# Attention scores from stacked float32r halves in two row groups instead of three bfloat16 parts, with smaller stack transfers and later expert loads

## The reference

```python
q, k, v = proj(Wq, bq), proj(Wk, bk), proj(Wv, bv)          # 16 heads x 2048 x 8
scores = einsum('bhqd,bhkd->bhqk', q, k) * (1 / sqrt(8))     # causal mask: -inf where k_pos > q_pos
p = softmax(scores);  out = einsum('bhqk,bhkd->bhqd', p, v) @ Wo.T + bo
x = layernorm(x + out)
x = layernorm(x + moe(x) + shared(x))                        # fp32 throughout
```

## Time and profile before

| what | value |
|---|---|
| median of 3 runs | 677.12 us (675.03 to 679.25) |
| span of the profiled execution | 662.1 us |
| PE busy | 559.1 us, 84% |
| DVE busy | 468.2 us, 71% |
| ACT busy | 356.9 us, 54% |
| mean granted TensorE clock | 0.914 of full speed |

### The profile page before, as it was taken

The page is one execution under the profiler, slowest core; times in us unless marked ns, Lnnn a source line. Parts: engine busy times, 40 slices in busy tenths (PEclk is TensorE's granted clock), DMA queues, the critical chain, the costliest instruction groups (busy, mean ns, idle before and its releaser), DMA issues.

```text
span 662.1 us, 10390 instructions
## 1 busy us (share of the span) xinstructions
PE 559.1 (84%) x3497; PEld 237.3 (36%) x3497; DVE 468.2 (71%) x765; ACT 356.9 (54%) x803; POOL 151.3 (23%) x267
## 2 busy tenths in 40 slices
PE   6244812999976999999999999999999899999890
PEld 3122401343422333344333333333333323665360
DVE  6933810789974898888888888788885333676674
ACT  2000301566551777767777777776778797332250
POOL 9600210221211022020101010110101325425453
PEclk9755765899995999999999999999999999999996
DMA  3221453000210000211000000000000101222133
GB/s 87 76 116 51 123 126 108 2 2 1 94 81 21 2 2 1 70 82 47 1 2 0 2 2 1 2 1 1 2 1 2 35 25 29 59 41 60 33 65 91
DMA packets 22204, 25.61 MB, mean 39 GB/s; under 512 B 2282, under 2 KB 20658, under 8 KB 21570
## 3 DMA queue, kind: packets, MB, share of 16 engines
q1 hardware_dynamic: 20192, 21.67, 10.2%
q0 software_dynamic: 1536, 3.15, 2.5%
q10 hardware_dynamic: 424, 0.13, 0.1%
HBM read 17.44 MB, written 7.21 MB: 37 GB/s over the span
## 4 chain that ended last, share of the span: by engine, by line
PE 67%; DVE 9%; SPq 7%; DMA 6%; issue 4%; POOL 3%; ACT 1%; POOLq 0%; DVEq 0%; ACTq 0%
PE out_ps L1291 20%; PE ring_ps L1274 17%; PE score_ps L1250 17%; SPq L619 5%; DMA k_stack<-parts_dram 4%; DVE part_max L986 3%; PE score_ps L1380 2%; PE score_ps L1253 2%; PE ring_ps L1397 1%; PE ring_ps L1300 1%; DVE qk_parts L965 1%; POOL k_stack L809 1%; DVE qk_parts L967 1%; PE score_ps L1332 1%; SPq L610 1%
## 5 line engine op out<-in xcount | busy, mean ns | idle before, releaser
L986 DVE TENSOR_REDUCE part_max<-score_ps 128x2 f32<-128x1024 f32 (+3 forms) x320 | 327.7, 1062 | 115.3 <-PE score_ps L1253 82.7
L863 ACT ACTIVATE probs<-ring_ps 128x512 f32<-128x512 f32 (+3 forms) x611 | 285.1, 537 | 157.0 <-PE ring_ps L1274 154.8
L1250 PE MATMUL score_ps<-k_stack,q_stack 96*128 96x512 bf16 (+3 forms) x640 | 183.7, 366 | 41.3 <-DMA k_stack<-parts_dram 29.2
L1274 PE MATMUL ring_ps<-q_stack,k_stack 96*128 96x512 bf16 (+3 forms) x611 | 173.5, 354 | 28.1 <-DMA q_stack<-max_rows 26.4
L1291 PE MATMUL out_ps<-probs,v_aug 128*32 128x512 f32 (+3 forms) x1280 | 153.5, 552 | 3.7 <-POOL probs L730 3.2
L1250 PEld LDWEIGHTS score_ps<-k_stack,q_stack 96*128 96x128 bf16 x640 | 60.9, 102 | 131.7 <-issue 58.8
L1274 PEld LDWEIGHTS ring_ps<-q_stack,k_stack 96*128 96x128 bf16 x611 | 52.6, 99 | 141.9 <-ACT probs L863 69.8
L730 POOL TENSOR_SCALAR_AFFINE_SELECT probs<-probs 128x512 f32<-128x512 f32 x64 | 40.6, 634 | 189.5 <-ACT probs L863 189.2
L1253 PE MATMUL score_ps<-mask_qk,ident_bf 128*128 128x128 bf16 x256 | 56.8, 241 | 0.0
L1291 PEld LDWEIGHTS out_ps<-probs,v_aug 128*32 128x32 f32 x1280 | 25.5, 109 | 49.7 <-issue 24.2
L741 POOL CAST max_parts<-row_max 128x16 bf16<-128x16 f32 x48 | 9.4, 196 | 146.1 <-DVE row_max L994 144.1
(11 more groups left out here) (179 smaller groups left out, 427.4 us busy)
## 6 DMA issues: line engine op xcount, KB each, us to landing
q_stack<-parts_dram SPq DMA_DIRECT2D x3, 1152.0 KB
k_stack<-parts_dram SPq DMA_DIRECT2D x9, 384.0 KB
parts_dram<-qk_parts SPq DMA_DIRECT2D x8, 384.0 KB, 2.5
sorted_dram<-q_stack SPq DMA_DIRECT2D x30, 64.0 KB, 1.5
x_sb<-in_L_attn_x_dram SPq DMA_DIRECT2D x4, 256.0 KB, 5.1
w_gu<-n_L_ffn_expert_gate_dram SPq DMA_DIRECT2D x1, 1024.0 KB, 26.6
w_gu<-in_L_ffn_expert_up_dram SPq DMA_DIRECT2D x1, 1024.0 KB, 11.7
wd<-n_L_ffn_expert_down_dram SPq DMA_DIRECT2D x8, 128.0 KB, 3.3
```

Of the source, the lines that this page charges most:

```text
L863: act.activation(probs[:, n % RING, 0:w], bank(it)[:, 0:w], ACT.Exp, scale=SCALE).then_inc(probs_ready, 1)
L986: dve.tensor_reduce(out=part_max[:, s % 2, t, 2 * hp:2 * hp + 2, c], in_=score_ps[:, m % 2, :, 0:w], axis=AX.X, op=ALU.max).then_inc(score ...
L1250: last = mm(score_ps[:, m % 2, i, 0:w], q_stack[0:KROWS, B % 2, h, t * P:(t + 1) * P], k_stack[0:KROWS, c, h, 0:w], start=True, stop=c < B)
L1274: mm(bank(it)[:, 0:w], k_stack[0:KROWS, j // TPB, h, j % TPB * P:(j % TPB + 1) * P], q_stack[0:KROWS, B % 2, h, skip:BLK], start=True, sto ...
```

## The change

- q and k are split into two float32r halves (ACT the first, DVE the second at once with one instruction, L962 before and L951 now); all 2 x 2 products make 32 rows, plus one row of -1 and two rows of maxima: 33 rows for the scores, 35 for the probabilities.
- Two heads share a stack row: head 2u in rows 0 to 63, head 2u + 1 in rows 64 to 127 (HALF = 64). The tensors keep their size in bytes per partition (8 pairs x 512 x 4 bytes).
- The two matmuls of a job read rows 0.. and rows 64..; the two mask matmuls of a masked job now come behind both.
- Stack transfers: q in four of 16 rows, k in two of 32 rows; each send is two transfers of 64 rows. Row maxima are placed with four transfers in place of one.
- Expert weights are loaded one expert at a time, three transfers behind the maxima of steps 5 to 13.
- The maxima are split in two steps on POOL, not five, and turned in float32.
- Rows read later by the mixture of experts (x1T, xs) lie elsewhere; three waits on q_sent and k_sent protect them.

```diff
-PARTS = 3
+HALVES = 2
+EXPERT_LOADS_AT = 5
-            clock["tensor"] += 0.84 * w + 8 + 107 * (c == B)
+            clock["tensor"] += 0.42 * w + 8 + 107 * (c == B)
...
-        q_stack = sb("q_stack", [P, 2, H, BLK], BF16)
-        k_stack = sb("k_stack", [P, NB, H, BLK], BF16)
+        q_stack = sb("q_stack", [P, 2, PAIRS, BLK], F32R)
+        k_stack = sb("k_stack", [P, NB, PAIRS, BLK], F32R)
...
-                sp.wait_ge(q_sent[b], 16)
-                rows = parts_dram[0, b].rearrange("a (o d h) t -> o (a d) h t", o=1, d=HD)[:, :, heads, :]
-                sp.dma_start(q_stack[0:STACK, b % 2, heads, :].rearrange("p h t -> p (h t)"),
-                             rows.rearrange("o p h t -> o p (h t)").to_broadcast(
-                                 [PARTS, PARTS * HD, (heads.stop - heads.start) * BLK])).then_inc(stacked, 16)
+                sp.wait_ge(q_sent[b], 32)
+                columns = slice(pairs.start * BLK, pairs.stop * BLK)
+                for j in range(2):
+                    for r in range(HALVES):
+                        at = HALF * j + r * HALVES * HD
+                        sp.dma_start(q_stack[at:at + HALVES * HD, b % 2, pairs, :].rearrange("p u t -> p (u t)").bitcast(F32),
+                                     parts_dram[0, b, j].rearrange("a d e -> d a e")[:, :, columns]).then_inc(stacked, 16)
...
+                for j in range(2):
+                    rows = parts_dram[1, b, j].rearrange("a (d o) e -> (a d) o e", o=1)[:, :, pairs.start * BLK:pairs.stop * BLK]
+                    sp.dma_start(k_stack[HALF * j:HALF * j + STACK, b, pairs, :].rearrange("p u t -> p (u t)").bitcast(F32),
+                                 rows.to_broadcast([HALVES * HD, HALVES, n])).then_inc(stacked, 16)
...
                     if s == 0:
-                        load_experts()
+                    if EXPERT_LOADS_AT <= s < EXPERT_LOADS_AT + NE:
+                        load_expert(s - EXPERT_LOADS_AT)
...
-                    dve.scalar_tensor_tensor(out=rest, in0=bank(it), scalar=bias_qk[:, side:side + 1], in1=parts[:, 0, :],
+                    dve.scalar_tensor_tensor(out=parts[:, 1, :], in0=bank(it), scalar=bias_qk[:, side:side + 1], in1=parts[:, 0, :],
                                              op0=ALU.add, op1=ALU.subtract).then_inc(qk_kept, 1)
-                    link(dve.tensor_copy(parts[:, 1, :], rest))
-                    link(dve.tensor_tensor(rest, rest, parts[:, 1, :], ALU.subtract))
-                    dve.tensor_copy(parts[:, 2, :], rest).then_inc((q_split, k_split)[side], 1)
...
                     for i in range(2):
-                        last = mm(score_ps[:, m % 2, i, 0:w], q_stack[0:KROWS, B % 2, h, t * P:(t + 1) * P],
-                                  k_stack[0:KROWS, c, h, 0:w], start=True, stop=c < B)
-                        if c == B:
+                        rows = slice(HALF * i, HALF * i + SCORE_ROWS)
+                        last = mm(score_ps[:, m % 2, i, 0:w], q_stack[rows, B % 2, 2 * g + hp, t * P:(t + 1) * P],
+                                  k_stack[rows, c, 2 * g + hp, 0:w], start=True, stop=c < B)
+                    if c == B:
+                        for i in range(2):
                             last = mm(score_ps[:, m % 2, i, w - P:w], ident_bf[:, :], mask_qk[:, :],
```

172 lines of the change are left out of this document (85 added, 87 removed).

## The result

The changed kernel takes 763.67 us (median of 4 runs, 751.18 to 782.15) beside 677.44 us of the kernel before (4 runs): it is slower, ratio 1.11 with a 95% interval of 1.105 to 1.115. The prediction was 588 us, so it failed in its direction.

The account below looks back on a forecast made before the run. PE was taken as the bound from 203.8 to 508. Savings of 15.9 + 13.0 + 26.3 + 3 + 8.8 + 27 = 94 gave span 568, with 15.0 around it 583, plus 5 for mutual waits 588 us; range 570 to 632.

Parts of the forecast that it names:

- Start, -15.9: Kernel start: shorter split and faster stack copies bring first scores at 20.0 instead of 35.9, saving 15.9 us.
- First hole, -13.0: Idle PE before 58: the other 1.5 MB of stacks lands by 28 to 31, saving 13.0 us.
- Second hole, -26.3: Idle PE before 112: expert loads issued behind step 5 no longer block the placing of maxima on SP, saving 26.3 us.
- rival of slow stacks: Stack copies stay at 80 GB/s because the sources of q are strided: 613 us, chance 0.07.
- 112 to 190 and the third hole, -3 and -8.8: DVE loses one block's casts, 3 us; block 2's stacks arrive before their first job near 203.8, saving 8.8 us.
- 203.8 to 508, -27: Long stretch where PE was full: overlapping pairs cut PE to 271, DVE then needs 277, saving 27 us.
- One pass each, 0.215: Long stretch: a float32r matmul of 512 columns takes one pass of 0.215 us, as bfloat16.
- rival of slow float32r: float32r streams at a float32 instruction's pace, 0.43 us for 512 columns: 731 us, chance 0.09.
- 9 us for changes: Long stretch: shape changes to mask matmuls and back in about 64 masked jobs cost PE 9 us.
- DVE becomes the bound: Long stretch: DVE needs 277 us against PE's 271, so DVE sets the pace.
- The rival with half the clock: PE falls to 1.2 GHz in the long stretch by idling more, needing 500 us; chance 0.04, including other slower causes.
- +15.0 around the span: Whole kernel: median time 677.1 is 15.0 us more than the profiled span of 662.1, added to the forecast span.

Follow-up runs that it names:

- e6_before_stacks: Kernel before, bfloat16, with expert loads spread behind steps 5 to 13 and stack copies cut to outermost dimensions 8 and 24: 607.92 us, ratio 0.919.
- e1_rows64: Changed kernel, but each score and probability matmul reads all 64 rows of its group instead of 33 and 35: 629.96 us, ratio 0.932.
- e9_half_max: Changed kernel with 64 rows read and the planner's old score cost of 0.84, DVE maxima reading half the columns: 625.94 us, ratio 0.924.
- e7_rows64_plan: Changed kernel with 64 rows per group read and the planner's score cost back at 0.84 per column: 612.38 us, ratio 0.924.

## Why the prediction was wrong, point by point

- **Start, -15.9: right to 1 us.** Scores at 20.98 (20.0 said), and k was split at 11.89 (11.9 said).
- **First hole, -13.0: nearly.** 4.67 us are left, so -10.3. k_stack lands last again, behind four q copies. The rate of the sends, which I took for a measure, is met where the stacks can be read alone: 160 GB/s in e6_before_stacks.
- **Second hole, -26.3: right in sum, one cause missed.** The hole is gone, but only 15 us of it hang on the expert loads; the rest was the slow stacks of block 1 ahead of the placing. Since both parts are in the change, the sum came out. In the rival of slow stacks I had left this hole closed; it would have stayed at about 11 us.
- **The four placings of maxima at 2.9 us: right** (2.54), and no one waits for them.
- **112 to 190 and the third hole, -3 and -8.8:** hidden by the clock in the kernel after. In e6_before_stacks, which has only the loads and the transfers, job 128 starts 56.8 us earlier than before, 3.0 of them at the first job; my three holes sum to 48.1. So these terms were sound. The 5.7 us beyond them aren't shown to be the transfers': that kernel is at full clock from 62 on, where before falls back from 87 to 121 and from 196 to 213.
- **203.8 to 508, -27: wrong three times over, even at full clock.** (1) "One pass each, 0.215": one pass is right, but the mean distance on the whole array is 0.254, because the weight load takes 0.19 instead of 0.10. The rows for it were there: 0.19 for a float32 load. The rival of slow float32r had the right sign at about a sixth of the price: 0.254 and not 0.43. (2) "9 us for changes": I priced the way to masks and forgot that each values quad and each transpose is a change too: 15 us more in the table's second and fourth line than before. (3) "DVE becomes the bound": it never did; PE stays the pace, with waits for ACT's banks worth up to 10.
- **The clock: the step that failed.** The sum held no term for the clock: "with 271 of 277 us of work I see no reason" took PE's busy share for what the clock follows. The earlier trace rows let me believe it: 0.5 where PE had stood still, 1.00 where it was busy. But every matmul in it used 96 or 128 rows; nothing had 33. In my sum the columns per us rose while the rows fell to a third, and I never multiplied the two. The Trainium skill ("TensorE: Matmul & The Clock Gate", "Part 1: The HAM clock gate") speaks of how busy the PE was and warns of idle gaps; here PE was busy 197.4 of 198.0 us at half clock, so the measurement decides against busy share as the measure. The price is the distance between the kernel after and e1_rows64: ratio 1.110 against 0.932, 0.18 of the time, some 120 us. e1_rows64 still stands some 43 us above the 588 (0.932 of 677.4 is 631), and of those the long stretch is 27 and the 91 us at half clock in front a part that no run isolates. The rival with half the clock named the level, but for a reason that didn't occur (PE idling more), and its 4% were far too few.
- **+15.0 around the span: a wrong reading.** In every profiled run here time and span differ by 1.7 to 2.0 us. What differs is the tail behind the start of the last unit: 100 us in the profile of before and in the four kernels run beside 662.4, but 112 to 116 in the kernel after and in the ten others, run beside 676 to 678. The surplus sits some 35 us before the end: the longest gap of PE in the last 100 us is 1.0 us in the five short tails and 2.6 to 4.9 in the others, and in e9_half_max PE is busy 4.1 of the ten us from 581 on, with nothing that the profile names to wait for. The kernel before has both values too, by its times. So it belongs to the occasion (the chip or its state), the profile had caught the short one, and its cause is open. For a ratio it hardly matters, but "what lies around" was a story for a number that I hadn't checked.

With all terms as measured, the change at full clock would have been worth what e1_rows64 and e7_rows64_plan show, 7 to 8%, not 13%.

## What to carry to other kernels

Before a change that packs fewer rows into a matmul, count the clock as a term of its own, for the time in which columns stream and for the rows they use; a full PE is no protection, and one kernel with the rows filled up to the end of the row group tells, for rows of zeros cost nothing that showed here and were worth 18% of the time. Price each passage between row groups, whole array and strips, and the weight load of the new format, before counting an overlap. And where a change has parts that can stand alone, the plain ones (how transfers are cut, what stands ahead of what in a queue) may carry all of the gain: here 8% against the 7 to 8% of the whole change at full clock, without touching a number format.
